# A graph attention and transformer kernel: masks moved to VectorE, the first product split in two parts, inputs in two buffers, edges written out in the loop's order

## The chip, the cores and the metric

The kernel runs on one core of a Trainium2 chip. TensorE (PE in the rows, PEld for its weight loads), VectorE (DVE), ScalarE (ACT), GpSimd (POOL) and SyncE (SP) each run their own stream of instructions in order and meet at semaphores. The metric is the device time of one execution, in microseconds (us); lower is better.

## What is computed

The input is a batch of 128 graphs of 128 nodes with 256 features. The first block is a graph attention with a top-16 filter, the second is three layers of graph attention with a feed-forward part of 1024 hidden units:

```python
h = jnp.maximum(_layernorm(x, axis=-1), 0.0)
x = x + _L0_gnn_ref(h, adj, W, a)
h = jnp.maximum(_layernorm(x, axis=-1), 0.0)
x = x + _L1_gnn_ref(h, adj, ...)

# _L0_gnn_ref
Wh = h @ W
e = leaky_relu((Wh @ a1)[:, :, None] + (Wh @ a2)[:, None, :], 0.2)
attention = softmax(where(adj > 0, e, -9e15))
attention = where(attention < 16th largest of its row, 0, attention)
return elu(attention @ Wh)

# _L1_gnn_ref, mask = adj + eye > 0, for each of three layers
scores = leaky_relu(si[:, :, None] + sj[:, None, :] + attn_b, 0.2)
attn = softmax(where(mask, scores, -inf))
h = layernorm(x + attn @ x) * g1 + beta1
x = layernorm(h + gelu(h @ W1 + b1) @ W2 + b2) * g2 + beta2
```

## The kernel before

**Tiling.** Four graphs make one group `k` (NG = 32 groups). A tile of scores is 128 x 512: the 128 nodes of four graphs side by side. For each group there is a first block (functions with `z_`, `e0`, `elu`) and three layers `l` of the second block. A pair (k, l) is a unit, and `seq(k, l)` is its number in the order of work: layer 1 of a group is worked one group behind layer 0, and layer 2 one more behind.

**Products in parts.** `mm1` (h @ W1, eight chunks `m` of 128 hidden units) and `mm2` (times W2) take float32r operands: each is split into a high part, rounded to float32r, and the low remainder, and three products are added: high by high, high by low, low by high. ScalarE makes the high part (`a_high`, `ht_high`), and the remainder comes from GpSimd for six of the eight chunks of `a_lo` and from VectorE for two (`LOW_ON_VECTOR = [3, 7]`) and for `ht_lo`. The product with W0 (`z_agg`) takes plain float32 operands, from `mixed`, which ScalarE copies out of PSUM in `mix_copy`. The aggregations (`agg`, `z_mix`) are plain float32 too.

**Masks.** `masks(k)` on VectorE makes two bf16 tiles with 0 or -2^100. One stays in SBUF for the first block; the other is parked in HBM by `park_mask` and loaded once for each layer by `load_mask`. The masks are added to the scores in PSUM, with a product by an identity at the end of `turn_sj` and `turn_e0`:

```python
pe.matmul(ps_s[:], ident_bf[:], mask_in[:, l].rearrange("p g m -> p (g m)"), start=False, stop=True, ...)
```

Then ScalarE forms a rectified copy (`leaky`), VectorE combines it with PSUM and takes the maximum (`scores_max`, `z_max`), ScalarE takes exponentials (`exps`), TensorE turns the result (`turn_p`, `turn_z`), and so on. `z_topk` finds the 16th largest value on VectorE before `turn_z`.

**Order.** Each engine has a function `iteration(i)`, an order written out by hand that works on pieces of groups i-3 to i+5. `schedule` calls it for i = -5 to 3 unrolled (the opening), for i = 4 to 25 in a loop on the chip whose body holds two iterations (11 turns), and for i = 26 to 34 unrolled (the closing). In the unrolled parts, pieces of groups that don't exist are left out. On TensorE one iteration holds 24 chunks of `mm1` and 24 of `mm2`, with the small products between them; `mm1` of a unit needs both halves of `ht_lo`, and `mm2` of chunk m needs that chunk's `a_lo`.

**Inputs.** `xr` is one buffer: `load_x(k)` waits until `elu_plus(k-1)` has read it. `zo` shares its memory with `hn0`, so `x0_norm(k)` waits for the first block's end for k-1. `elu_plus`, `elu_exp` and `elu_minus` work on all four graphs at once.

Of the kernel before, what the change touches and what calls it, by code (L numbers as in the profile page):

```python
# [12 lines left out]
P = 128  # L13
D = 256
# [12 lines left out]
FIRST, LAST = -5, NG + 3  # L27
# [55 lines left out]
def before_last(k, l):  # L83


    if isinstance(k, At):
        return seq(k, l) - 1
    at = L * k + (L + 1) * l - 1
    return sum(L * kk + (L + 1) * ll < at for kk in range(NG) for ll in range(L))
# [8 lines left out]
def chunks_before(k, l, m):  # L98


    c = seq(k, l) * MC + m
    if isinstance(k, At):
        return c - 2
    same = [seq(kk, ll) * MC + mm for kk in range(NG) for ll in range(L) for mm in range(MC) if (ll * MC + mm) % 3 == (l * MC + m) % 3]
    return max([n + 1 for n in same if n < c], default=0)
# [14 lines left out]
def build_program(nc, x, adj, W0, a0, attn_w, attn_b, W1, b1, W2, b2, g1, be1, g2, be2, out):  # L120
    ctx = ExitStack()
    with ctx:
# [8 lines left out]

        w1_hi = sb("w1_hi", [L, DC, HID], F32R)
# [3 lines left out]
        w0 = sb("w0", [DC, D])  # L136
# [12 lines left out]
        ident_bf = sb("ident_bf", [P], BF16)  # L149
# [14 lines left out]
        xr = sb("xr", [G, D])  # L164
# [23 lines left out]
        top = sb("top", [TOPK_ROUNDS, G, 8])  # L188
        w1_stage = X[:, 1:3].rearrange("p l g d -> p (l g d)").rearrange("p (c n) -> p c n", c=DC)
# [36 lines left out]
        CONSTS = 10  # L226
# [6 lines left out]
        def flat(ap):  # L233
            return ap.rearrange("p a n -> p (a n)")

        def schedule(iteration, eng):

            for i in range(FIRST, FIRST_STEADY):
                iteration(i)
# [3 lines left out]
            for i in range(LAST_STEADY + 1, LAST):  # L243
                iteration(i)
# [5 lines left out]
        def _(sp):  # L250
# [10 lines left out]
            sp.dma_start(xr[:], x_g[0]).then_inc(s["x_in"], 16)  # L261
            sp.dma_start(a0_row, row(a0.rearrange("n o -> (n o)"), 2 * D).rearrange("p (j d) -> p j d", j=2)).then_inc(s["a0_in"], 16)
# [1080 lines left out]
```

## Time and profile before

| | |
|---|---|
| median of 3 runs | 2915.42 us (2913.39 to 2915.62) |
| the profiled execution: its time, its span | 2913.98 us, 2912.3 us |
| mean granted TensorE clock | 0.986 of 2.4 GHz |
| busy: TensorE, its weight loads | 2752.7 us (95%), 2474.2 us (85%) |
| busy: VectorE, ScalarE, GpSimd | 2026.0 us (70%), 2350.6 us (81%), 2313.8 us (79%) |
| mean HBM traffic | 29 GB/s |

The span runs from the first to the last instruction; the time is 1.7 us longer. Busy shares are averages over the opening, the loop and the closing, which have different limits. Matmuls are pipelined: the duration of one in the rows holds its way through the array, and what it costs is the distance from its start to the next start. One float32 product of two operands appears as two MATMUL records, a float32r or bf16 product or a transpose as one.

### The profile page before, as it was taken

Reading aid. Unit: us, or ns where it says so; the run is one execution under the profiler, and the core shown is the slowest. Engines: PE = TensorE matmul, PEld = TensorE weight load, DVE = VectorE, ACT = ScalarE, POOL = GpSimd, SP = SyncE. Lnnn points to the kernel's source line nnn. Section 1 sums busy time; section 2 is a strip of 40 time slices with the busy share of each in tenths; the row PEclk is TensorE's granted clock in tenths of the full one; section 3 lists DMA queues with packets and bytes.
Section 4 is the critical chain, followed back from the end, with each engine's and each line's share of the span. In section 5 each row is a group of like instructions: output and inputs, shape, how many; then the busy total and the mean of one; then the engine's idle time right before and its main releaser. Section 6 shows DMA issues by size and latency. Waiting matters only on the chain.

```text
span 2912.3 us, 58716 instructions
## 1 busy us (share of the span) xinstructions
PE 2752.7 (95%) x17636; PEld 2474.2 (85%) x17636; DVE 2026.0 (70%) x7283; ACT 2350.6 (81%) x4767; POOL 2313.8 (79%) x2410
## 2 busy tenths in 40 slices
PE   4689999999999999999999999999999999999995
PEld 3578998888888898988889898888888999999874
DVE  4767777767777777777777777776777777676542
ACT  3577888888898888888888888888888888887663
POOL 0466888888888888888888888888888888888874
PEclk9899999999999999999999999999999999999997
DMA  4100011101101101101110110111110111010001
GB/s 150 46 28 26 25 34 25 34 20 34 33 27 25 35 20 34 34 26 34 25 35 20 34 32 28 25 34 20 34 35 25 34 25 34 20 30 19 10 10 15
DMA packets 96432, 89.72 MB, mean 31 GB/s; under 512 B 9120, under 2 KB 94368, under 8 KB 96032
## 3 DMA queue, kind: packets, MB, share of 16 engines
q1 hardware_dynamic: 79136, 68.32, 7.6%
q0 software_dynamic: 16896, 16.78, 4.4%
q8 instruction: 163, 2.67, 0.4%
q14 instruction: 237, 1.94, 0.2%
HBM read 47.34 MB, written 37.75 MB: 29 GB/s over the span
## 4 chain that ended last, share of the span: by engine, by line
PE 79%; DVE 12%; issue 4%; ACT 3%; POOL 1%; SPq 0%; DMA 0%; DVEq 0%; POOLq 0%; ACTq 0%
PE ps_ff L1120 11%; PE ps_ff L1122 10%; PE ps_ff L1121 10%; PE ps_mm L1101 10%; PE ps_mm L1099 10%; PE ps_mm L1100 10%; PE ps_ag L1157 5%; PE ps L1233 4%; PE ps_ht L1171 3%; PE ps L1223 2%; DVE U L893 1%; PE ps_s L1145 1%; DVE H L1005 1%; DVE st_y_six L789 1%; PE ps_s L1134 1%
## 5 line engine op out<-in xcount | busy, mean ns | idle before, releaser
L418 POOL TENSOR_TENSOR a_lo<-A,a_hi 128x512 fp32r<-128x512 f32 x576 | 776.1, 1350 | 347.3 <-ACT a_hi L541 334.9
L1120 PE MATMUL ps_ff<-w_hi,a_hi 128*128 128x256 f32 x3072 | 900.6, 293 | 26.3 <-DVE a_lo L995 14.6
L1121 PE MATMUL ps_ff<-w_lo,a_hi 128*128 128x256 f32 x3072 | 853.5, 278 | 0.0
L1122 PE MATMUL ps_ff<-w_hi,a_lo 128*128 128x256 f32 x3072 | 852.8, 278 | 0.0
L533 ACT ACTIVATE A<-ps_mm,b_col 128x512 f32<-128x512 f32 x768 | 521.7, 683 | 319.9 <-PE ps_mm L1101 191.9
L1099 PE MATMUL ps_mm<-ht_hi,w_hi 128*128 128x512 f32 x1536 | 630.8, 411 | 4.8 <-ACT A L533 3.4
L1120 PEld LDWEIGHTS ps_ff<-w_hi,a_hi 128*128 128x128 f32 x3072 | 577.4, 188 | 54.8 <-DVE a_lo L995 17.3
L1101 PE MATMUL ps_mm<-ht_lo,w_hi 128*128 128x512 f32 x1536 | 607.0, 395 | 0.0
L1100 PE MATMUL ps_mm<-ht_hi,w_lo 128*128 128x512 f32 x1536 | 604.2, 393 | 0.0
L1121 PEld LDWEIGHTS ps_ff<-w_lo,a_hi 128*128 128x128 f32 x3072 | 578.5, 188 | 18.4
L1122 PEld LDWEIGHTS ps_ff<-w_hi,a_lo 128*128 128x128 f32 x3072 | 578.1, 188 | 0.0
L541 ACT ACTIVATE a_hi<-A 128x512 fp32r<-128x512 f32 x768 | 478.2, 631 | 14.4
L935 DVE CUSTOM_DVE_ANT_0 junk<-X,wij_row 128x256 bf16<-128x256 f32 x768 | 342.5, 509 | 11.8 <-POOL X L442 6.7
L1101 PEld LDWEIGHTS ps_mm<-ht_lo,w_hi 128*128 128x128 f32 x1536 | 289.7, 189 | 62.4
L1099 PEld LDWEIGHTS ps_mm<-ht_hi,w_hi 128*128 128x128 f32 x1536 | 290.0, 189 | 54.6 <-ACT A L533 5.2
L1100 PEld LDWEIGHTS ps_mm<-ht_hi,w_lo 128*128 128x128 f32 x1536 | 290.7, 189 | 44.7
L986 DVE TENSOR_TENSOR ht_lo<-ps_ht,ht_hi 128x512 fp32r<-128x512 f32 x192 | 130.6, 680 | 259.9 <-ACT ht_hi L614 259.7
L425 POOL TENSOR_TENSOR H<-H,g_row 128x512 f32<-128x512 f32 x192 | 267.8, 1402 | 12.7 <-ACT H L547 12.3
L397 POOL TENSOR_TENSOR H<-X,g_row 128x512 f32<-128x512 f32 x192 | 261.8, 1377 | 17.9 <-DMA out<-H 9.8
L408 POOL TENSOR_TENSOR H<-H,bb_row 128x512 f32<-128x512 f32 x192 | 275.0, 1432 | 0.0
L1005 DVE TENSOR_TENSOR H<-ps_ff,H 128x512 f32<-128x512 f32 x192 | 123.0, 682 | 178.7 <-PE ps_ff L1122 176.9
L970 DVE SCALAR_TENSOR_TENSOR X<-ps_ag,a_rden,X 128x256 f32<-128x256 f32 x384 | 167.1, 476 | 105.7 <-PE ps_ag L1157 104.7
(113 smaller groups left out, 5129.8 us busy)
## 6 DMA issues: line engine op xcount, KB each, us to landing
xr<-in_x SPq DMA_DIRECT2D x32, 512.0 KB, 3.9
out<-x SPq DMA_DIRECT2D x32, 512.0 KB, 2.9
out<-H POOLq DMA_DIRECT2D x32, 512.0 KB, 6.1
mask_in<-mask_park SPq DMA_DIRECT2D x96, 128.0 KB, 2.4
adj_sb<-in_adj SPq DMA_DIRECT2D x32, 256.0 KB, 2.9
mask_park<-mask_out SPq DMA_DIRECT2D x32, 128.0 KB, 1.7
X<-in_L_gnn_W SPq DMA_DIRECT2D x3, 1024.0 KB, 5.7
H<-in_L_gnn_W SPq DMA_DIRECT2D x3, 1024.0 KB, 6.7
```

What stands on the lines that cost most here:

```text
L408: pool.tensor_tensor(H[:, l, two], H[:, l, two], bb_row[:, l:l + 1, :].to_broadcast([P, 2, D]), ALU.add).then_inc(s["h_res"], 1)
L418: pool.tensor_tensor(a_lo[:, at], A[:, at], a_hi[:, at].bitcast(F32), ALU.subtract).then_inc(s["a_lo_gpsimd"], 1)
L425: pool.tensor_tensor(H[:, l, two], H[:, l, two], g2_row[:, l:l + 1, :].to_broadcast([P, 2, D]), ALU.mult).then_inc(s["y_scaled"], 1)
L533: act.activation(A[:, (l * MC + m) % 3], ps_mm[m % 2][:], ACT.Gelu, bias=b1_col[:, l, m:m + 1]).then_inc(s["gelu_made"], 1)
L541: act.activation(a_hi[:, at], A[:, at], ACT.Copy).then_inc(s["a_hi_made"], 1)
L935: last = dve.tensor_tensor_reduce(out=junk[:, 2 * g + j], in0=X[:, l, g], in1=wij_row[:, l, j], scale=1.0, scalar=0.0, op0=ALU.mult, op1=A ...
L1099: pe.matmul(ps_mm[m % 2][:], w1_hi[:, l, d, cols], ht_hi[:, k % 2, d], start=(d == 0), stop=False)
L1100: pe.matmul(ps_mm[m % 2][:], w1_lo[:, l, d, cols], ht_hi[:, k % 2, d], start=False, stop=False)
L1101: last = pe.matmul(ps_mm[m % 2][:], w1_hi[:, l, d, cols], ht_lo[:, k % 2, d], start=False, stop=(d == DC - 1))
L1120: pe.matmul(out_g, a_hi[:, at, cols], w2_hi[:, l, m], start=first, stop=False, skip_group_check=True)
L1121: pe.matmul(out_g, a_hi[:, at, cols], w2_lo[:, l, m], start=False, stop=False, skip_group_check=True)
L1122: last = pe.matmul(out_g, a_lo[:, at, cols], w2_hi[:, l, m], start=False, stop=final, skip_group_check=True)
```

## The change

1. **Masks.** The mask products leave `turn_sj` and `turn_e0`, with `ident_bf`. Two new functions on VectorE, `scores_mask(k, l)` and `z_mask(k)`, add the mask in SBUF to the rectified copy, before `scores_max` and `z_max`.
2. **W0.** W0 is split once into `w0_hi` and `w0_lo`. `mix_copy` becomes `mix_high` (the same copy, into float32r), a new `mix_low` on VectorE makes the remainder from PSUM, and `z_agg` adds three float32r products.
3. **Inputs and aliases.** `xr` has two buffers; `load_x` runs one group further ahead. `z_out` writes into `x1`, so `x0_norm` no longer waits for the ELU. The ELU works in halves (`elu_exp(k, half)`, `elu(k, half)`). `kept` is also `pt0`, and serves as scratch with `U0`. Several global semaphores become one for each layer, and `moments` waits for the old coefficients before its first instruction and not before its second group.
4. **Buffers of units.** `ht_hi`, `ht_lo` and the ring of three `A`, `a_hi`, `a_lo` are now picked by the unit's number in the order of work. In the loop that gives the same choice.
5. **Order.** All engines have a new order in the loop, and the opening and the closing are written out (functions `opening` and `closing`) in nearly that order. The low parts stay split two to six. SP loads W0, a0, W2 and W1 of layer 0 ahead of x(0), and adj(0) comes after all constants and x(1); constants have three semaphores in place of one.

```diff
-                pe.matmul(ps_s[:], ident_bf[:], mask_in[:, l].rearrange("p g m -> p (g m)"), start=False, stop=True,
-                          skip_group_check=True).then_inc(s["sj_turned"], 1)
...
+            def scores_mask(k, l):
+                if not here(k):
+                    return
+                n = seq(k, l)
+                dve.wait_ge(s["scores_leaky"], value(n + 1))
+                dve.wait_ge(s_mask[l], value(k * 16 + 16))
+                tt(flat(U[:]), flat(U[:]), flat(mask_in[:, l]), ALU.add).then_inc(s["masked"], 1)
...
+            def z_mask(k):
+                if not here(k):
+                    return
+                dve.wait_ge(s["z_leaky"], value(k + 1))
+                dve.wait_ge(s["mask_made"], value(k * 2 + 1))
+                tt(flat(U0[:]), flat(U0[:]), flat(mask0[:]), ALU.add).then_inc(s["z_masked"], 1)
...
+            def mix_low(k, half):
+                if not here(k):
+                    return
+                dve.wait_ge(s["mix_hi_made"], value(k * 2 + half + 1))
+                tt(flat(mix_lo[:]), ps_0[:], flat(mix_hi[:]).bitcast(F32), ALU.subtract).then_inc(s["mix_split"], 1)
...
-                pe.wait_ge(s["mix_copied"], value(k * 2 + half + 1))
+                pe.wait_ge(s["mix_split"], value(k * 2 + half + 1))
                 for g in range(2):
...
-                        last = pe.matmul(ps_0[:, g * D:(g + 1) * D], mixed[:, c, g * P:(g + 1) * P], w0[:, c],
-                                         start=(g == 0 and c == 0), stop=(g == 1 and c == DC - 1), skip_group_check=True)
+                        pe.matmul(out_g, mix_hi[:, c, rows], w0_hi[:, c], start=(g == 0 and c == 0), stop=False, skip_group_check=True)
+                        pe.matmul(out_g, mix_hi[:, c, rows], w0_lo[:, c], start=False, stop=False, skip_group_check=True)
+                        last = pe.matmul(out_g, mix_lo[:, c, rows], w0_hi[:, c], start=False, stop=(g == 1 and c == DC - 1),
+                                         skip_group_check=True)
```

The order in the loop, where the prediction speaks of it (k = i+2 has its first block in this iteration):

```diff
 TensorE, from the end of layer 1's mm2 to turn_z and z_agg:
                 mm2(i - 1, 1, 7)
-                mm1(i - 2, 2, 1)
                 mm1(i - 2, 2, 2)
                 mm1(i - 2, 2, 3)
+                turn_sj(i, 1)
                 mm2(i - 2, 2, 0)
                 mm1(i - 2, 2, 4)
+                mm1(i - 2, 2, 5)
                 mm2(i - 2, 2, 1)
                 turn_z(i + 2)
-                mm1(i - 2, 2, 5)
+                turn_h(i + 1, 0, 0)
+                mm2(i - 2, 2, 2)
                 z_mix(i + 2, 0)
-                turn_h(i + 1, 0, 0)
                 mm1(i - 2, 2, 6)
                 z_agg(i + 2, 0)
 VectorE, the same stretch:
                 y_sum(i - 1, 1)
                 y_moments(i - 1, 1)
-                z_recip(i + 2)
                 z_topk(i + 2)
+                z_recip(i + 2)
+                a_low(i - 2, 2, 3)
+                scores_mask(i, 1)
+                ht_low(i + 1, 0, 0)
                 scores_max(i, 1)
-                a_low(i - 2, 2, 3)
-                ht_low(i + 1, 0, 0)
+                mix_low(i + 2, 0)
+                recip(i, 1)
                 z_out(i + 2, 0)
 VectorE, the end of an iteration and (after the bar) the start of the next:
-                ht_low(i, 1, 0), y1_sum(i - 1, 2, 0), ht_low(i, 1, 1) | scores_max(i + 2, 0), y1_sum(i - 1, 2, 1)
+                ht_low(i, 1, 0) | y1_sum(i - 1, 2, 0), scores_mask(i + 2, 0), scores_max(i + 2, 0), ht_low(i, 1, 1)
 TensorE, the same place:
-                mm2(i + 1, 0, 7), mm1(i, 1, 2), mm1(i, 1, 3) | mm2(i, 1, 0)
+                turn_h(i, 1, 1), agg(i - 1, 2, 1), mm2(i + 1, 0, 5) | mm1(i, 1, 0), mm1(i, 1, 1)
```

## Rows read from the trace of the kernel before

**Rows 1.** The page: busy time (share) xinstructions, and the chain that ended last.
```profile
PE 2752.7 (95%) x17636; PEld 2474.2 (85%) x17636; DVE 2026.0 (70%) x7283; ACT 2350.6 (81%) x4767; POOL 2313.8 (79%) x2410
...
PE 79%; DVE 12%; issue 4%; ACT 3%; POOL 1%; SPq 0%; DMA 0%; DVEq 0%; POOLq 0%; ACTq 0%
```

**Rows 2.** Windows: length; busy (x) of PE, PEld, DVE, ACT, POOL; PEclk, DMA share, GB/s.
```profile
0.00:103.00 103.00, 49.63 (x205) 41.48 (x206) 55.50 (x188) 36.99 (x74) 14.67 (x29) 0.95 0.40 123
103.00:300.00 197.00, 169.75 (x1021) 147.85 (x1020) 139.70 (x535) 142.19 (x304) 122.43 (x138) 0.92 0.09 28
...
616.00:2250.00 1634.00, 1602.85 (x10422) 1448.29 (x10420) 1195.91 (x4316) 1395.26 (x2834) 1383.34 (x1425) 1.00 0.12 29
2250.00:2586.00 336.00, 335.38 (x2186) 303.81 (x2184) 245.28 (x906) 292.16 (x595) 287.61 (x301) 1.00 0.12 29
2586.00:2912.30 326.30, 283.36 (x1784) 251.14 (x1782) 157.40 (x511) 210.10 (x409) 240.56 (x242) 0.93 0.09 14
```

**Rows 3.** Timeline of PE in a loop group: `turn_z`, `z_agg`, `mm2`. Start, length (us).
```profile
1501.04 0.66 PE L1210 MATMUL ps<-ident,U 128*128 128x128 f32 x4 [0.72 <-DVE U L893]
1501.45 0.48 PE L1099 MATMUL ps_mm<-ht_hi,w_hi 128*128 128x512 f32 x1
...
1505.65 1.89 PE L1233 MATMUL ps<-w,mixed 128*128 128x256 f32 x8
...
1507.49 0.28 PE L1121 MATMUL ps_ff<-w_lo,a_hi 128*128 128x256 f32 x1
...
1510.00 0.28 PE L1122 MATMUL ps_ff<-w_hi,a_lo 128*128 128x256 f32 x1
```

**Rows 4.** Timeline of PE in another loop group: a mask product.
```profile
1561.09 0.38 PE L1202 MATMUL ps<-mask,ident_bf 128*128 128x512 bf16 x1
...
1561.43 0.28 PE L1121 MATMUL ps_ff<-w_lo,a_hi 128*128 128x256 f32 x1
```

**Rows 5.** Waits in the loop (616 to 2250): us in total, times, longest.
```profile
PEld ps L1210 <- DVE U L893: 16.0, 19, 1.0
...
PE ps_ff L1120 <- DVE a_lo L995: 12.2, 9, 1.5
...
PE ps_ff L1120 <- issue: 6.4, 9, 1.0
```

**Rows 6.** Groups of DVE in the loop: busy us, mean ns.
```profile
L970 DVE SCALAR_TENSOR_TENSOR X<-ps_ag,a_rden,X 128x256 f32<-128x256 f32 x230 | 100.0, 475 | 57.8 <-PE ps_ag L1157 57.8
L995 DVE TENSOR_TENSOR a_lo<-A,a_hi 128x512 fp32r<-128x512 f32 x115 | 91.1, 792 | 33.9 <-ACT a_hi L541 33.4 <-PE ps_ff L1122 0.5
...
L986 DVE TENSOR_TENSOR ht_lo<-ps_ht,ht_hi 128x512 fp32r<-128x512 f32 x114 | 77.4, 679 | 134.4 <-ACT ht_hi L614 134.4
```

**Rows 7.** Three lines by source: duration ns min/median/max.
```profile
L995 DVE TENSOR_TENSOR a_lo<-A,a_hi x192: 656/692/1857, 117.0 to 2889.4; 128x512 fp32r<-128x512 f32 x192
...
L986 DVE TENSOR_TENSOR ht_lo<-ps_ht,ht_hi x192: 655/682/693, 97.0 to 2866.1; 128x512 fp32r<-128x512 f32 x192
...
L418 POOL TENSOR_TENSOR a_lo<-A,a_hi x576: 1256/1300/1829, 108.6 to 2889.0; 128x512 fp32r<-128x512 f32 x192
```

**Rows 8.** Timeline of DVE: the chain to `turn_z`, and the loop's branch.
```profile
1114.24 0.29 DVE L949 CUSTOM_DVE_ANT_0 U<-ps_s,U 128x128 f32<-128x128 f32 x1 [2.46 <-issue]
...
1492.08 1.29 DVE L1005 TENSOR_TENSOR H<-ps_ff,H 128x512 f32<-128x512 f32 x2 [3.45 <-PE ps_ff L1122]
...
1498.82 2.16 DVE L893 SCALAR_TENSOR_TENSOR U<-U,top 128x128 f32<-128x128 f32 x4
```

**Rows 9.** Chain that ended last, in the opening: the first weights.
```profile
16.05 7.07 DMA X<-in_L_gnn_W
23.17 7.00 PE ps_ht L1180 x32
```

**Rows 10.** Timeline of ACT in the opening.
```profile
42.63 1.91 ACT L521 ACTIVATE w_hi<-H 128x2048 fp32r<-128x2048 f32 x1 [1.86 <-DMA H<-in_L_gnn_W]
44.45 0.58 ACT L656 ACTIVATE pt<-ps 128x512 f32<-128x512 f32 x1
```

More of the change, by code:

```diff
@@ L65, in here @@
     return isinstance(k, At) or 0 <= k < NG
+UNITS = sorted(((k, l) for k in range(NG) for l in range(L)), key=lambda u: L * u[0] + (L + 1) * u[1])
 def seq(k, l):
@@ L72, in seq @@
         return k * L + ((L + 1) * l - L)
-    at = L * k + (L + 1) * l
-    return sum(L * kk + (L + 1) * ll < at for kk in range(NG) for ll in range(L))
+    return UNITS.index((k, l))
 def earlier(k, l):
@@ L83, in before_last, with ht_at, a_at @@
 def before_last(k, l):
[L86 to L89, printed above, removed]
+    return seq(k, l) - 1 if isinstance(k, At) else max(seq(k, l) - 1, 0)
+def ht_at(k, l):
+    return k % 2 if isinstance(k, At) else (seq(k, l) + 1) % 2
+def a_at(k, l, m):
+    return ((L + 1) * l * MC + m) % 3 if isinstance(k, At) else (seq(k, l) * MC + m) % 3
 def ready(k, l):
@@ L101, in chunks_before @@
     c = seq(k, l) * MC + m
[L102 to L105, printed above, removed]
+    return c - 2 if isinstance(k, At) else max(c - 2, 0)
 def some(n):
@@ L219, in build_program @@
         s_w2 = [sem(f"w2_in{l}") for l in range(L)]
+        s_xin = [sem(f"x_in{p}") for p in range(2)]
         s_mask = [sem(f"mask_in{l}") for l in range(L)]
@@ L231, in row, with schedule @@
             return ap.rearrange("(o n) -> o n", o=1).to_broadcast([P, n])
[L233 to L239, printed above, removed]
+        def schedule(opening, iteration, closing, eng):
+            opening()
             with eng.Fori(0, (LAST_STEADY + 1 - FIRST_STEADY) // 2) as j:
@@ L242, in schedule @@
                 iteration(At(j, 2, FIRST_STEADY + 1))
-            for i in range(LAST_STEADY + 1, LAST):
-                iteration(i)
+            closing()
         block = ctx.enter_context(nc.Block())
@@ L338, in _ @@
+            schedule(opening, iteration, closing, sp)
             sp.wait_ge(s["out_added"], 16 * NG)
@@ L509, in _ @@
+            schedule(opening, iteration, closing, pool)
         @block.scalar
@@ L714, in iteration @@
                 a_high(i - 1, 1, 1)
+                p_copy(i + 1, 0)
                 h_norm(i - 2, 2)
@@ L762, in _ @@
+            schedule(opening, iteration, closing, act)
         @block.vector
@@ L902, in z_out @@
                 dve.wait_ge(s["z_agg"], value(n + 1))
-                for g in range(2):
-                    j = 2 * half + g
-                    last = ts(zo[:, j], ps_0[:, g * D:(g + 1) * D], zrden[:, j:j + 1], None, ALU.mult)
-                last.then_inc(s["z_out_made"], 1)
-            def elu_plus(k):
-                if not here(k):
-                    return
-                dve.wait_ge(s["z_out_made"], value(k * 2 + 2))
                 if some(k):
@@ L1083, in _ @@
+            schedule(opening, iteration, closing, dve)
         @block.tensor
         def _(pe):
-            pe.wait_ge(s["const_made"], 5)
+            pe.wait_ge(s["const_made"], 4)
             def mm1(k, l, m):
@@ L1323 @@
+            schedule(opening, iteration, closing, pe)
 _INS = ["x", "adj", "L0_gnn_W", "L0_gnn_a", "L1_gnn_attn_w", "L1_gnn_attn_b", "L1_gnn_W1", "L1_gnn_b1",
```

3148 lines of the change are left out of this document (2885 added, 263 removed).

## The prediction

> **What bounds the kernel now.** I read the page first: TensorE is busy 95% of the span and makes 79% of the chain that ended last; VectorE, ScalarE and GpSimd are at 70, 81 and 79% [rows 1]. An average hides the stages, so next the windows, cut at starts of `turn_e0` [rows 2]. The loop from 616 to 2250 us holds 19 groups, 86.0 us each, and PE is idle in 31 us of 1634. The four unrolled groups after it take 84.0 us each with 0.6 us idle. The first 300 us leave PE idle for 53 + 27 us and the last 326 us for 43. So in the loop the time is TensorE's own work, and what TensorE loses is lost at the edges. ScalarE and GpSimd are 85% busy in the loop (1395 and 1383 of 1634), VectorE 73%: 63 us a group.
>
> The third view is PE's timeline, because a matmul's duration is not its cost. `mm2` products start 0.114 us apart (22 steps from 1507.49 to 1510.00) [rows 3]. A mask product with one `mm2` product behind it takes from 1561.09 to 1561.43, 0.34 us, so it costs 0.226 us [rows 4]. One half of `z_agg`, eight float32 records, with one `mm2` product behind it takes from 1505.65 to 1507.49, 1.84 us, so it costs 1.73 [rows 3].
>
> The fourth is the list of waits in the loop [rows 5]. PE's queue waits for VectorE before `turn_z` in every one of the 19 groups, 16.0 us in all (0.84 each), and at nine loop turns for an `a_lo` of VectorE (12.2 us) and for its own branch ("issue", 6.4 us).
>
> **What the change takes from TensorE.** (a) Four mask products a group, three layers and the first block, 128 in all: 128 x 0.226 = 28.9 us. (b) `z_agg`: eight float32 records become twelve float32r products of the shape that `mm2` has, 12 x 0.114 = 1.37 us in place of 1.73. 64 halves x 0.36 = 23.0 us. Together 51.9 us, 1.6 us a group. TensorE is the bound in 27 groups, and at the edges these pieces stand in the chain as well, so I count all of it. From below it could be worth 27/32 of that, 44 us.
>
> **What it puts on VectorE.** Four mask adds a group, 128x512 with both inputs in SBUF. The nearest row is the `a_lo` remainder, also from SBUF: mean 0.79 us, from 0.66 to 1.86 [rows 6, 7]. I take 0.8, bounds 0.66 and 1.86. Two `mix_low` a group, one input in PSUM, as `ht_lo`: 0.68, never over 0.69 [rows 6, 7]. Sum 4 x 0.8 + 2 x 0.68 = 4.6 us a group; the ELU in halves adds a few tenths. VectorE goes from 63 to 68 us in a period of about 84, 80%. Hidden behind TensorE as long as no step that TensorE waits for comes later than its place in the order.
>
> The spread of that `a_lo` row needs a reason: the same subtraction with one input in PSUM keeps to 0.655 to 0.693, with both in SBUF it reaches 1.857, and GpSimd's own `a_lo` reaches 1.829 over a median of 1.300 [rows 7]. So the mask adds will sometimes wait for GpSimd, and GpSimd for them. The Trainium skill (SBUF — State Buffer, "SBUF: two separate sides") says that VectorE with two SBUF inputs and GpSimd share a port pair as an exclusive lock, the loser blocked for the whole instruction. The trace agrees with a blocking of about one such operation at most. By that rule an add behind a whole `a_lo` of GpSimd (1.30) would take 1.96, and four of them a group 7.8 us in place of my 3.2; that is taken up in the second rival.
>
> **What moves in the loop.** (c) `turn_z`. From the start of `y_sum` at 1492.08 to the end of `z_topk` at 1500.98, VectorE runs without a gap to speak of, 8.9 us, and PE waits for its end [rows 3, 8]. The y_sum itself starts when `mm2(i-1,1,7)` ends. Between that and `turn_z` the new order has the same six units of `mm1` and `mm2` and now also the four transposes of `turn_sj` (0.41 us, the distance from 1501.04 to 1501.45 [rows 3]), and `z_recip` (0.14) comes after `z_topk`. So the wait of 0.84 falls to about 0.3: 0.5 x 31 groups = 16 us off. Bounds 0 and 0.84. (d) `z_agg(0)` now waits for two steps, `mix_high` and then `mix_low`, and one `mm1` chunk (about 1.4 us) stands between. From `z_mix`'s last start: 0.3 through the array (the rest of its duration), 0.58 on ScalarE as `z_copy` [rows 10], 0.68 on VectorE, small hops, about 1.7; PE covers 1.4. A wait of 0.3 x 31 = 9 us on, bounds 0 and 1 each if `scores_max`, which stands ahead of `mix_low`, is late. The second half has 5 us of cover. (e) The loop's turn. VectorE stands idle 2.46 us at its branch [rows 8]. Before, that fell after both `ht_lo` of the unit; now it falls between them, with `y1_sum` (2 x 0.475 less overlap, 0.87 [rows 6]), a mask add (0.8) and `scores_max` (about 1) ahead of the second. From the first `ht_lo`'s start: 0.7 + 2.5 + 0.9 + 0.8 + 1 + 0.7 = 6.6 us, PE's cover (two `mm2` chunks, transposes, `agg`, one `mm2` chunk, less ScalarE's lead) some 5. A wait of 1.6 at each of 11 turns, where before 12.2 + 6.4 over 9 turns gave 2.1 [rows 5]. PE's own branch has shorter work queued ahead, which can eat the difference. I take 0, bounds -10 and +20 us.
>
> SP: `load_adj(i+3)` now stands behind `load_x(i+4)`, which waits for the ELU late in iteration i. `masks` follows in the next iteration after more than ten operations, so the adjacency has time to land. `store_x1` and the mask loads stand behind waits that were met an iteration earlier. I cost them at nothing; if the cover went, `masks` and behind it VectorE's whole order would be late by a transfer, 3 to 5 us a group.
>
> **The edges.** Before, the first weights are issued at 16.05, land at 23.1, and their 32 bias products hold PE to 30.2, ahead of the first `turn_e0` [rows 9]; then `z_copy` stands behind `w2_high(1)`, which ends at 44.5, some 3 us after `turn_z` [rows 10]. Now W1 and W2 are issued ahead, but x(0) behind 2.5 MB and adj(0) behind some 6 MB. At the rate of the first weights and constants I put adj(0) near 23 us, so the first `turn_e0` comes about where it was, and only the 3 us of `w2_high(1)` are won: -3 us, bounds -12 and +8. In the dependent stretches of opening and closing, some eight turns of the score chain stand open to PE, and each is longer by a mask add less a mask product (0.6) or two `mix_low` less 0.7: +6 us, bounds 2 and 12.
>
> **The sum.** Span 2912.3 - 51.9 (a, b) - 16 (c) + 9 (d) + 0 (e) - 3 + 6 = 2856.4; with 1.7 around it 2858. The runs' median is 1.4 above the profiled execution's 2913.98. I add 2 us for small waits as VectorE fills up and say **2861 us**, 1.9% faster.
>
> **The rivals.**
> *The new order takes out more.* PE's idle time in the loop (31 us) mostly goes and the opening wins its 12 us: 2861 - 15 - 9 - 5 = 2832. For it: each wait in the list has a cause that an order can mend. Against it: the branches stay.
> *VectorE's new work shows.* The mask add sits in the chain `leaky`, add, `scores_max`, `exps`, `turn_p`, and PE takes `turn_p` at a fixed place. If the adds are blocked by GpSimd (1.86 each) and half of 4 x 1.86 + 2 x 0.68 = 8.8 us a group reaches PE in 27 groups, that is +119: 2980; a quarter gives 2921, slower than before. It decides at 57/27 = 2.1 us of new waits a group. Against it: no wait of PE for `exps` is among those of the loop, and VectorE has 23 us of slack a group.
> *Most is given back.* (d) costs 1 us a group (+22), the loop's turn +20, opening +8: about 2900.
> *No change.* The three products of `z_agg` don't start 0.114 apart and the mask products were free. Against it: [rows 3, 4] show both prices on PE's own clock of starts. 2912.
>
> **How the numbers follow.** Forecast 0.55, more taken out 0.18, given back 0.13, VectorE shows 0.11 (0.02 of it within 0.2%), no change 0.03. A measurement of this kernel tells some 0.2%, 6 us, from nothing. Faster 0.55 + 0.18 + 0.13 = 0.86, same 0.02 + 0.03 = 0.05, slower 0.09. The range leaves out a little at each end: from the low case less 4, 2828, to the given-back case, 2900. The likeliest case alone is 2842 to 2880.
>
> **What would show it.** In the trace after: no bf16 matmuls; `z_agg` at 0.114 a product; windows of the loop near 84.3 us a group, PE busy still over 97%; VectorE near 80%; `turn_z` waiting 0.3 us or less for VectorE, a new wait of 0.2 to 0.4 at `z_agg`; mask adds of 0.7 to 0.9 mean with a tail to 1.9. Wrong if PE waits for `exps` or `ht_lo` in each group, or if the first `mm1`, at 103 us before, starts after 110.

## The result, and the profile after

The changed kernel took 3005.6 us (median, 3003.5 to 3007.1) beside 2914.4 us for the kernel before: a ratio of 1.0314, 95% interval 1.0301 to 1.0327, so 3.1% slower. The prediction was 2861 us, faster, with a range of 2828 to 2900. The profiled execution took 3003.48 us with a span of 3001.7.

The page of the kernel after, the lines that answer [rows 1]: busy time and the chain.

```profile
PE 2760.5 (92%) x17764; PEld 2459.4 (82%) x17764; DVE 2231.2 (74%) x7574; ACT 2366.1 (79%) x4800; POOL 2295.3 (76%) x2409
...
PE 41%; DVE 21%; issue 14%; POOL 10%; ACT 10%; DMA 0%; DVEq 0%; POOLq 0%; ACTq 0%
```

TensorE was 79% of the chain and is 41%. The time is no longer TensorE's own work. That its busy time has not fallen by the 52 us says little, because behind a wait a matmul's record is longer: 0.49 us for the `mm1` product that ends a wait at 1693.00, 0.40 for its like at 1693.80. Where the waits are gone, the busy time does fall with the work moved: 2763.4 us in z4, 2722.4 in z2 (two runs below that differ by that work alone).

Windows of the kernel after. The last three are cut at the same starts of `turn_e0` as in [rows 2]; the first two end at the first `mm1` (106, before 103) and at the fifth `turn_e0` (290, before 274), so the second has no partner in [rows 2] (length; busy of PE, PEld, DVE, ACT, POOL; clock; DMA; GB/s).

```profile
0.00:106.00 106.00, 49.90 (x219) 44.65 (x220) 57.60 (x199) 37.76 (x77) 10.84 (x28) 0.98 0.40 121
106.00:290.00 184.00, 145.94 (x856) 126.79 (x856) 131.21 (x477) 120.90 (x262) 103.03 (x116) 0.88 0.10 30
...
638.00:2324.00 1686.00, 1607.96 (x10490) 1434.10 (x10489) 1319.91 (x4484) 1402.91 (x2850) 1370.68 (x1426) 0.99 0.12 28
2324.00:2667.00 343.00, 334.80 (x2207) 300.50 (x2207) 279.38 (x944) 295.09 (x601) 285.47 (x301) 1.00 0.12 27
2667.00:3001.70 334.70, 286.00 (x1790) 252.75 (x1788) 168.56 (x526) 214.67 (x414) 241.23 (x244) 0.93 0.09 14
```

The 19 groups of the loop take 1686 us against 1634 (88.7 each against 86.0), the four behind it 343 against 336, the closing 8 us more, and the loop's window begins 22 us later. VectorE is busy 69.5 us a group in the loop (1319.9 / 19), about the 68 forecast.

TensorE's waits in the loop, 638 to 2324 us (us in total, times, longest), to be read against [rows 5], and VectorE's wait before `recip`. [rows 5] has the wait of `turn_z` on the weight loads' row (PEld), 16.0 us; on the row of the products (PE), as here, the kernel before had 12.2 us in the same 19 groups.

```profile
PE ps_mm L3043 <- issue: 22.8, 14, 2.9
PE ps_ff L3066 <- DVE a_lo L2403: 16.3, 13, 1.3
PE ps_ag L3101 <- DVE X L2378: 14.0, 25, 1.2
PE ps_ff L3066 <- POOL a_lo L507: 6.8, 12, 0.7
PE ps L3152 <- DVE U L2289: 5.4, 9, 1.2
...
PE ps L3178 <- DVE mix_lo L2297: 3.3, 5, 0.7
```

```profile
DVE a_rden L2368 <- ACT U L1198: 58.9, 29, 2.8
```

The wait of `turn_z` (L3152) fell as forecast. Three others came: for TensorE's own branch, for `a_lo`, and at `agg` for `y1_sum` (L2378). And VectorE, the engine that got more to do, stands idle 58.9 us before `recip` in the loop, where the kernel before lost 2.8 us in the whole run.

How a branch reaches TensorE: VectorE, then TensorE, at one turn of the loop (start, length, idle before).

```profile
1685.04 0.69 DVE L2394 TENSOR_TENSOR ht_lo<-ps_ht,ht_hi 128x512 fp32r<-128x512 f32 x1 [1.79 <-ACT ht_hi L1216]
1688.14 0.88 DVE L2378 SCALAR_TENSOR_TENSOR X<-ps_ag,a_rden,X 128x256 f32<-128x256 f32 x2 [2.41 <-issue]
```

```profile
1689.07 1.13 PE L3101 MATMUL ps_ag<-X,pt 128*128 128x256 f32 x4 [1.11 <-DVE X L2378]
...
1693.00 0.49 PE L3043 MATMUL ps_mm<-ht_hi,w_hi 128*128 128x512 f32 x1 [1.42 <-issue]
...
1695.79 0.50 PE L3043 MATMUL ps_mm<-ht_hi,w_hi 128*128 128x512 f32 x1 [1.13 <-issue]
```

VectorE is idle 2.41 us at its branch, as it was before (2.46) [rows 8]. Behind it stands a `y1_sum` that `agg` waits for, so the loss reaches TensorE at once. Then TensorE stands idle twice more, 1.42 and 1.13 us before `mm1`, and waits for nothing that the profile shows. I read both as its own branch: with the loop written out (y5 below) this row is gone.

### The profile page after: what moved, and what is told of

It is laid out like the page before. It is cut to its first block, busy times and chain, and to the rows that moved or that the text cites. A ratio compares the mean times of both kernels' runs of the same rounds, so it can differ in the third digit from the quotient of the medians.

```text
span 3001.7 us, 59533 instructions
## 1 busy us (share of the span) xinstructions
PE 2760.5 (92%) x17764; PEld 2459.4 (82%) x17764; DVE 2231.2 (74%) x7574; ACT 2366.1 (79%) x4800; POOL 2295.3 (76%) x2409
## 4 chain that ended last, share of the span: by engine, by line
PE 41%; DVE 21%; issue 14%; POOL 10%; ACT 10%; DMA 0%; DVEq 0%; POOLq 0%; ACTq 0%
PE ps_ff L3066 6%; PE ps_ff L3067 6%; PE ps_ff L3068 6%; PE ps_mm L3043 5%; DVE junk L2335 5%; PE ps_mm L3045 5%; PE ps_mm L3044 5%; PE ps_ag L3101 3%; POOL a_lo L507 3%; ACT H L1150 2%; ACT a_hi L1144 2%; DVE X L2378 2%; DVE st_h_six L2178 2%; ACT A L1136 2%; POOL H L497 1%
## 5 line engine op out<-in xcount | busy, mean ns | idle before, releaser
L3066 PE MATMUL ps_ff<-w_hi,a_hi 128*128 128x256 f32 x3072 | 887.0, 289 | 44.4 <-DVE a_lo L2403 26.1
L3043 PE MATMUL ps_mm<-ht_hi,w_hi 128*128 128x512 f32 x1536 | 630.1, 410 | 41.0 <-issue 24.6
L2335 DVE CUSTOM_DVE_ANT_0 junk<-X,wij_row 128x256 bf16<-128x256 f32 x768 | 342.2, 508 | 17.3 <-POOL X L531 12.2
L2403 DVE TENSOR_TENSOR a_lo<-A,a_hi 128x512 fp32r<-128x512 f32 x192 | 196.3, 1022 | 156.5 <-ACT a_hi L1144 146.6
L497 POOL TENSOR_TENSOR H<-H,bb_row 128x512 f32<-128x512 f32 x192 | 253.3, 1325 | 10.0 <-DVE bb_row L2166 9.9
L1150 ACT ACTIVATE H<-H,st_y_nmr,st_y_rstd 128x256 f32<-128x256 f32 x384 | 198.7, 590 | 56.9 <-POOL st_y_nmr L450 56.9
L3101 PE MATMUL ps_ag<-X,pt 128*128 128x256 f32 x768 | 209.8, 396 | 28.0 <-DVE X L2378 23.0
```

Source lines behind the costliest of these rows:

```text
L497: pool.tensor_tensor(H[:, l, two], H[:, l, two], bb_row[:, l:l + 1, :].to_broadcast([P, 2, D]), ALU.add).then_inc(s_res[l], 1)
L2335: last = dve.tensor_tensor_reduce(out=junk[:, 2 * g + j], in0=X[:, l, g], in1=wij_row[:, l, j], scale=1.0, scalar=0.0, op0=ALU.mult, op1=A ...
L3043: pe.matmul(ps_mm[m % 2][:], w1_hi[:, l, d, cols], ht_hi[:, ht_at(k, l), d], start=(d == 0), stop=False)
L3066: pe.matmul(out_g, a_hi[:, at, cols], w2_hi[:, l, m], start=first, stop=False, skip_group_check=True)
L3101: last = pe.matmul(ps_ag[:, g * D:(g + 1) * D], pt[:, j * P:(j + 1) * P], X[:, l, j], start=(g == 0), stop=(g == 1), skip_group_check=True)
```

## The experiments

Medians in us, ratio to runs of the kernel before on the same chip with its 95% interval. "Old" is the kernel before, "new" the kernel after, with the edit named.

| run | edit | time | ratio |
|---|---|---|---|
| x1 | old + masks and W0 as after | 3031.2 | 1.0399 (1.0382 to 1.0417) |
| x2 | new, masks and W0 as before | 3004.5 | 1.0309 (1.0292 to 1.0326) |
| x3 | old + masks alone | 3050.5 | 1.0472 (1.0454 to 1.0489) |
| x4 | old + W0 alone | 2948.3 | 1.0123 (1.0106 to 1.0140) |
| y5 | new, loop written out | 2931.6 | 1.0062 (1.0046 to 1.0079) |
| y6 | old, loop written out | 2875.4 | 0.9872 (0.9856 to 0.9888) |
| y7 | new, branch moved | 2981.0 | 1.0231 (1.0214 to 1.0248) |
| y8 | new, `recip` late | 2985.1 | 1.0242 (1.0225 to 1.0259) |
| z1 | new, branch moved, `recip` late | 2942.9 | 1.0097 (1.0081 to 1.0114) |
| z2 | new, written out, `recip` late | 2879.1 | 0.9878 (0.9862 to 0.9894) |
| z3 | old + masks, written out | 2924.4 | 1.0026 (1.0008 to 1.0044) |
| z4 | z2, masks and W0 as before | 2903.7 | 0.9964 (0.9954 to 0.9975) |
| w1 | new, masks added in PSUM | 2991.6 | 1.0267 (1.0242 to 1.0292) |
| w2 | x3, masks added in PSUM | 2953.5 | 1.0137 (1.0119 to 1.0154) |
| w3 | z2, masks in PSUM, one step of the opening | 2866.8 | 0.9843 (0.9827 to 0.9860) |
| w4 | z1, masks in PSUM | 2946.5 | 1.0122 (1.0105 to 1.0139) |
| v1 | old, masks in PSUM, W0, written out | 2911.3 | 1.0002 (0.9993 to 1.0011) |
| v2 | v1 with the loop | 2952.4 | 1.0135 (1.0114 to 1.0156) |

### Work or order: x1 to x4

x1 puts the added work into the old order (here the masks; `mix_low` and the split of W0 likewise), x2 takes it out of the new one.

```diff
 x1, VectorE
+                scores_mask(i + 1, 0)
                 scores_max(i + 1, 0)
...
+                mix_low(i + 2, 0)
                 ht_low(i + 1, 0, 0)
...
                 ht_low(i + 1, 0, 1)
+                mix_low(i + 2, 1)
```

> The kernel before, its order unchanged, with the masks added on VectorE (each add directly ahead of its maximum) and W0 in high and low parts (the low part of the first half ahead of ht_low(i+1,0,0), the second behind ht_low(i+1,0,1)). Theory Work (VectorE's new instructions are what TensorE waits for): the 52 us taken from TensorE come back as waits of the size seen after the change, about 4 us a group, so 2914 - 52 + 27 x 4.4 = 2980, at least 2940. Theory Order (the new order of the steps makes the waits): the work is nearly hidden as forecast, 2914 - 52 + 20 for waits of the score chain and of z_agg = 2882, at most 2900.

> The kernel after, with its order, buffers and edges, but the masks added by products on TensorE again and W0 in plain float32 (no scores_mask, z_mask, mix_low). Theory Work: without the new instructions on VectorE the waits go, and the time is that of the kernel before or a little less, 2895 to 2920. Theory Order: TensorE has 52 us more to do and waits as it did after the change, so 3005 + 52 less what the longer TensorE work covers (about half): 3030, at least 2990.

> The kernel before with the masks alone on VectorE; W0 stays float32. Theory Work, if the mask adds carry it (they lie in the score chain and are blocked by GpSimd's port): 2914 - 29 + 27 x 3 = 2966, above 2930. Theory Order: 2914 - 29 + some 10 = 2895.

> The kernel before with W0 in two parts alone; masks stay products on TensorE. Forecast of term (b) and (d): 2914 - 23 + 9 = 2900 by both theories; under 2895 if the wait of z_agg is covered in the old order, over 2915 if ht_low behind mix_low is late for mm1.

Neither theory stands alone. In the old order the work costs 117 us, above what theory Work said; and the new order costs 90 us with the old work. Together they cost 91, not 207: in the new order the new work is free of cost (3004.5 against 3005.6), but free of gain too. In x2 VectorE stands idle 89 us before `recip` in the 19 groups of the loop, so that wait comes with the order and not with the work. x3 came out on theory Work's side, but 84 us above its number: the masks alone cost 137 us. W0 alone costs 34 where 14 were to be won; the time is in the range that x4 gave to a late `ht_low`, but TensorE waits for `mix_low` there, as shown below.

TensorE's waits of x3 between 616 and 2290 us show where (the rows of [rows 5] for this kernel).

```profile
PE ps_ff L1137 <- DVE a_lo L1008: 34.9, 28, 2.8
PE ps L1223 <- DVE U L898: 30.3, 9, 3.7
PE ps_ff L1137 <- issue: 18.5, 10, 2.1
```

The count 9 is that of the loop's turns in this window: `turn_z` waits up to 3.7 us for VectorE once a turn and not in the groups between. From one `turn_e0` to the next, x3 takes 98 us in a group with a turn, 85 in one without and 85 to 86 behind the loop.

### The loop's branch: y5, y6, y7, z3

```diff
 y5, y6, z3: schedule
-            with eng.Fori(0, (LAST_STEADY + 1 - FIRST_STEADY) // 2) as j:
-                iteration(At(j, 2, FIRST_STEADY))
-                iteration(At(j, 2, FIRST_STEADY + 1))
+            for i in range(FIRST_STEADY, LAST_STEADY + 1):
+                iteration(i)
 y7: VectorE, first calls of the body moved to its end (TensorE: seven calls, up to mm1(i - 1, 1, 3))
-                y1_sum(i - 2, 2, 0)
-                scores_mask(i + 1, 0)
-                scores_max(i + 1, 0)
-                ht_low(i - 1, 1, 1)
                 y1_sum(i - 2, 2, 1)
...
                 ht_low(i, 1, 0)
+                y1_sum(i - 1, 2, 0)
+                scores_mask(i + 2, 0)
+                scores_max(i + 2, 0)
+                ht_low(i, 1, 1)
```

> The kernel after with its loop on the chip written out: the same calls in the same order for i = 4 to 25, no branch. In the trace after, the groups with a loop turn take about 92.6 us from turn_e0 to turn_e0 and the four behind the loop 85.3. Theory Turn (an overfull VectorE can't make good what it loses at its branch): the turn's excess of 7.3 us goes 11 times, 3005 - 80 = 2925, at most 2945. Theory Spread (the waits are those of every group, the turn only moves them): at least 2980.

> The kernel before with its loop written out. Its groups with a turn take 87.1 us, the others 84.9 in the loop and 84.1 behind it, so 11 x 3.0 + 11 x 0.8 = 42 off by the four groups behind the loop: 2872; at least 11 x 2.2 = 24 off: 2890. Theory Turn expects the gap of the two written-out kernels to be 2925 - 2872 = 53 us or less, against 91 with the loops; theory Spread the same 91.

> The kernel after with the loop's branch at the place in the order where it was before: on VectorE behind ht_low(i,1,1), on TensorE behind mm1(i,1,3). The order of the instructions is unchanged. If the new place of the branch makes the turn dear (term (e), put at 0 with an upper bound of 20): some 5 of the 7.3 us a turn come back, 3005 - 55 = 2950. If the turn is dear wherever it stands, since VectorE has no slack behind it to catch up: 2990 to 3010; the masks alone in the old order, with the branch at its old place, speak for that.

> The old order with the masks on VectorE (3050 with the loop), the loop written out. Its groups with a turn took 98 us, the four behind the loop 84.9 to 86. Theory Turn: 3050 - 11 x 13 = 2907, which is 2875 and some 30. Theory Spread (blocked adds cost in every group): at least 2950.

Eleven turns of the loop cost 74 us after (3005.6 - 2931.6) and 39 before (2914.4 - 2875.4). The gap of the two kernels falls from 91 to 56. From one `turn_e0` to the next, the kernel after takes 92.5 us in a group with a turn and 85.3 in one without, and y5 takes 85.3 in all, so the price is paid where the branch is. The kernel before has 87.2 and 84.9, y6 has 84.2. Written out, a kernel also loses the loop's counter and address instructions (y5 has 55,386 instructions, the kernel after 59,533), and no run separates these from the branch. "Branch" stands for both below.

With the branch at its old place 25 us come back (y7), half of what was expected, so the place is a part of it. With the masks in the old order the turns cost 126 us (3050.5 - 2924.4), 87 more than without; theory Turn put z3 17 us too low, and 49 us over y6 remain without a branch. The eight executions of z3 spread over 27 us (2908.8 to 2936.1), so these numbers are good to some 10 us.

Windows from the fifth `turn_e0` to the last (27 groups), and behind it: y5, then y6.

```profile
288.50:2590.80 2302.30, 2259.13 (x14906) 2028.18 (x14905) 1886.24 (x6372) 1992.12 (x4050) 1924.18 (x2023) 1.00 0.12 29
2590.80:2923.50 332.70, 283.24 (x1787) 250.46 (x1785) 167.09 (x526) 214.15 (x413) 241.31 (x244) 0.94 0.09 14
```

```profile
273.20:2545.40 2272.20, 2271.65 (x14799) 2058.18 (x14798) 1658.74 (x6130) 1974.89 (x4024) 1945.25 (x2025) 1.00 0.12 29
2545.40:2868.70 323.30, 280.13 (x1785) 248.64 (x1783) 156.97 (x511) 210.23 (x409) 240.25 (x242) 0.95 0.09 14
```

Without branches the old kernel is TensorE alone, 84.2 us a group with 0.5 us idle in 27 groups. The new one has less to do there and takes 85.3, with 43 us idle. The edges are 15.3 + 9.4 us longer.

### The wait for the exponentials: y8, z1, z2, z4

```diff
 y8, z1, z2, z4: VectorE, in the opening, the loop and the closing
-                recip(i + 1, 0)
                 masks(i + 2)
                 y_sum(i, 0)
...
+                recip(i + 1, 0)
                 y1_sum(i + 1, 0, 0)
```

> The kernel after with each recip(k, l) directly ahead of y1_sum(k, l, 0) and not ahead of z_out, masks and y_sum, in the opening, the loop and the closing. VectorE waits 58 us for exps there in the loop. If these waits (the order) reach TensorE, half of them come back, 3005 - 40 = 2965. If the added work carries it, VectorE only waits elsewhere: 2995 to 3010.

> The kernel after with both single edits: the branch at its old place on VectorE and TensorE (alone 25 us off) and recip directly ahead of y1_sum (alone 20 us off). If the two are different causes they add: 3005 - 25 - 20 = 2960. If both only give VectorE back the same slack: no better than 2975. If a VectorE with no idle time for exps recovers from its branch as fast as before (3 us a turn): 2940.

> The kernel after with the loop written out (alone 2931) and recip directly ahead of y1_sum. In the run with recip late the groups behind the loop take 83.8 us against 85.3: 2931 - 27 x 1.4 = 2893. If the wait for exps is covered where no branch is: 2925.

> The new order with the old work (mask products on TensorE, W0 in float32), written out and with recip late: it differs from the kernel after with the same two edits by the moved work alone. If terms (a) and (b) hold where no branch and no early recip stand in the way: that kernel's time + 52 - 10 = about 2935. If VectorE's new work gives it all back even here: the same time, 2893.

What it takes away, in VectorE's timeline of the kernel after, behind the loop:

```profile
2531.64 0.18 DVE L2368 RECIPROCAL a_rden<-a_den 128x4 f32<-128x4 f32 x1 [2.79 <-ACT U L1198]
2531.82 0.88 DVE L2310 TENSOR_SCALAR x<-ps,z_rden 128x256 f32<-128x256 f32 x2
```

`recip` needs the exponentials (L1198) and only `y1_sum`, some operations on, needs `recip`; `z_out`, `node_scores` and `ht_low` stand behind it meanwhile. How it reaches TensorE: the wait for `a_lo` in 19 groups without a branch, y5 (638 to 2240 us), then z2 (616 to 2290).

```profile
PE ps_ff L3065 <- DVE a_lo L2402: 18.3, 19, 1.1
```

```profile
PE ps_ff L3065 <- DVE a_lo L2402: 0.6, 1, 0.6
```

Moved, `recip` is worth 20 us with the loop (y8), 38 with the branch moved too (y7 to z1), and 52.5 written out (y5 to z2). So the branch hides a part of the gain. A turn does not become cheaper by it: the eleven cost 106 us with `recip` late (y8 against z2) and 74 without, and at the old place 64 (z1 against z2) and 49 (y7 against y5). One cause can be read in y8: the moved `recip` is now the first call of the body, behind the branch, `y1_sum` waits for it there, and `agg` waits 22.6 us in the loop in place of 14.0. In z1 both stand ahead of the branch, and the two edits together give 63 us, more than 20 + 25.

y8 missed its 40 us by half. z1 fell on the number of its third expectation (2940), but that one wanted turns of 3 us and they cost 5.8, so the number was met by luck. z2 beat its own by 14 us, and z4 lies between its two.

z4 and z2 differ by the moved work alone. Windows of the 27 groups: z4, then z2, then w3 of the next part.

```profile
284.40:2565.70 2281.30, 2280.19 (x14797) 2060.48 (x14796) 1612.10 (x6210) 1992.58 (x4051) 1892.15 (x2023) 1.00 0.12 29
```

```profile
288.50:2544.10 2255.60, 2242.33 (x14905) 2025.13 (x14904) 1807.42 (x6372) 1987.52 (x4051) 1926.36 (x2023) 1.00 0.12 29
```

```profile
287.00:2531.20 2244.20, 2238.64 (x14906) 2025.89 (x14905) 1728.88 (x6372) 1989.50 (x4051) 1899.39 (x2024) 1.00 0.12 29
```

The moved work is worth 24.6 us (2903.7 - 2879.1), and 0.95 us a group (84.5 to 83.5), of the 1.6 that terms (a) and (b) take from TensorE. With unblocked adds (w3) it is 1.4.

z4 against y6 shows the rest of the change, since both do the old work without a branch and without an early `recip`: 2903.7 against 2875.4, 28 us more. By the profiled spans 9 us of it lie in the 27 groups (2281.3 against 2272.2) and 22 in the edges. So no run shows the new order ahead of the old one at the same work.

### The port: w1 to w4

```diff
-                tt(flat(U[:]), flat(U[:]), flat(mask_in[:, l]), ALU.add).then_inc(s["masked"], 1)
+                tt(ps_s[:], ps_s[:], flat(mask_in[:, l]), ALU.add).then_inc(s["masked"], 1)
...
-                tt(flat(U0[:]), flat(U0[:]), flat(mask0[:]), ALU.add).then_inc(s["z_masked"], 1)
+                tt(ps_0[:], ps_0[:], flat(mask0[:]), ALU.add).then_inc(s["z_masked"], 1)
 w3, the opening
-                w2_low(2)
                 mix_low(1, 1)
+                w2_low(2)
```

> The kernel after, but scores_mask and z_mask add the mask to the scores in PSUM (in place, behind the rectified copy) and not to the copy in SBUF; scores_max adds the two as before, so the sum is the same. The adds then have one SBUF input. After the change they took 0.91 (96) and 1.49 us (32), with a minimum of 0.67. Theory Port (they are blocked while GpSimd works, and block it): each takes 0.67 to 0.70 with no tail, VectorE gets back 96 x 0.22 + 32 x 0.8 = 47 us, and 3005 falls to 2960 to 2975. Theory Count (it is the number of instructions and their places, not the blocking): 2995 to 3010.

> The old order with the masks alone on VectorE (3050), the adds done in PSUM. There the score adds took 1.34 us each in the run with both edits. Theory Port: VectorE gets back about 96 x 0.65 + 32 x 0.4 = 75 us, most of it within 30 us behind the branch, so the 13 us that a turn costs fall to 6: 3050 - 80 = 2970 or less. Theory Count: 3030 to 3050.

> The kernel after, written out, recip late (2879), with the adds in PSUM, and in the opening mix_low(1,1) ahead of w2_low(2), for which z_agg waited 2.4 us there. Theory Port: the groups fall from 83.5 us to TensorE's 82.9, 27 x 0.6 = 16 off, the opening 3 to 5 off: 2860. Theory Count: 2875.

> The kernel after with its loop, the branch at its old place and recip late (2943), the adds in PSUM. Theory Port: the turn's 4 us fall to 2 and the groups by 0.6: 2943 - 22 - 16 = 2905. Theory Count: 2935 to 2943.

By source, min/median/max in ns. The kernel after: `z_mask`, `scores_mask`, `mix_low`, `a_low` on VectorE.

```profile
L2249 DVE TENSOR_TENSOR U<-U,mask x32: 673/1624/1659, 33.0 to 2671.2; 128x512 f32<-128x512 f32 x32
...
L2348 DVE TENSOR_TENSOR U<-U,mask_in x96: 662/691/1793, 73.8 to 2932.9; 128x512 f32<-128x512 f32 x96
...
L2297 DVE TENSOR_TENSOR mix_lo<-ps,mix_hi x64: 675/684/693, 45.7 to 2708.9; 128x512 fp32r<-128x512 f32 x64
...
L2403 DVE TENSOR_TENSOR a_lo<-A,a_hi x192: 654/693/1823, 124.0 to 2979.6; 128x512 fp32r<-128x512 f32 x192
```

`scores_mask` in the old order, in SBUF (x3) and in PSUM (w2):

```profile
L953 DVE TENSOR_TENSOR U<-U,mask_in x96: 684/1548/1877, 74.9 to 2980.2; 128x512 f32<-128x512 f32 x96
```

```profile
L953 DVE TENSOR_TENSOR ps_s<-ps_s,mask_in x96: 673/700/700, 74.7 to 2896.5; 128x512 f32<-128x512 f32 x96
```

With one input in PSUM the tail is gone. In the old order that alone takes 97 us off (w2), so most of what the masks cost there was GpSimd's blocking. In the new order the score adds were mostly unblocked already (median 691), and it is worth 14 us in w1, whose four executions spread over 21, 12 with a step of the opening (w3), and nothing measurable in w4. So the port explains x3, and only a small part of the kernel after. `z_mask` was blocked nearly always, here by a bias operation of GpSimd, which is then late itself: VectorE, then GpSimd, of the kernel after.

```profile
2586.19 1.53 DVE L2249 TENSOR_TENSOR U<-U,mask 128x512 f32<-128x512 f32 x1
```

```profile
2585.88 1.29 POOL L524 TENSOR_TENSOR H<-H,be_row 128x512 f32<-128x512 f32 x1
2587.13 1.73 POOL L531 TENSOR_TENSOR X<-H,be_row 128x512 f32<-128x512 f32 x1
```

The add ends 0.55 us after the GpSimd operation that had begun before it, and the next one of GpSimd takes 1.73 us where its median is 1.29. The Trainium skill (SBUF — State Buffer, "SBUF: two separate sides") has this rule, a lock on the pair of ports held for a whole instruction, between a GpSimd operation that reads SBUF and a VectorE operation with two SBUF inputs; w2 agrees, with 700 ns at most for an add that has one.

### The old order once more: v1, v2

```diff
 v1, v2: the kernel before with W0 and the masks in PSUM; v1 written out. TensorE:
+                mm2(i - 2, 2, 2)
                 z_agg(i + 2, 0)
-                mm2(i - 2, 2, 2)
```

> The old order, buffers and edges, written out, with the masks added by VectorE in PSUM, W0 in two parts, and z_agg(i+2,0) one chunk of mm2 later, so that its wait of 2 us for mix_low is covered. Written out, the old kernel took 2875 with TensorE at 84.1 us a group. If TensorE keeps what is taken from it (1.6 us a group) where the adds are not blocked, no branch stands in the way and the edges are the old ones: 2875 - 27 x 1.4 = 2837; if, as in the new order, half is given back: 2855. Not better than 2867 (the best of the new order) if the new order is what makes the moved work fit.

> The same kernel with the loop. The masks in PSUM alone took 2953, of which some 11 x 6 for the turns beyond those of before. The turn should stay dear, at about 9 us against 2.3 to 3 before, even with unblocked adds: v1 + 80 = 2920 to 2940. If the turn becomes as cheap as before: v1 + 38 = 2875 to 2890.

Both missed. TensorE's waits of v1 between 616 and 2290 us have one row, and VectorE's timeline in one group says why:

```profile
PE ps L1265 <- DVE mix_lo L913: 35.9, 20, 1.8
```

```profile
1002.73 0.47 DVE L996 SCALAR_TENSOR_TENSOR X<-ps_ag,a_rden,X 128x256 f32<-128x256 f32 x1
1003.12 0.68 DVE L1012 TENSOR_TENSOR ht_lo<-ps_ht,ht_hi 128x512 fp32r<-128x512 f32 x1
1003.71 0.68 DVE L913 TENSOR_TENSOR mix_lo<-ps,mix_hi 128x512 fp32r<-128x512 f32 x1
```

The cover was put before the wrong half. It is the second `z_agg` that waits, 1.8 us in each of 20 groups, for a `mix_low` that stands behind `ht_low` and `y1_sum`. The same wait is in x4 (28.7 us in 19 groups), where it carries most of what W0 alone lost. So v1 doesn't show what the old order could do with that wait mended, and whether it would beat w3 is open. The 41 us between v1 and v2 are again the branch: 3.7 us a turn, near the 3.5 of the kernel before and far from the 11.5 with blocked adds, as the second expectation of v2 had it for the difference.

## Why the prediction was wrong, step by step

**The sum that the runs give.** 91.2 us = 35.0 (the branch: 74.0 against 39.0) + 52.5 (`recip` ahead of its need, y5 to z2) + 3.7 (all the rest, z2 against y6: by the windows 28 us of longer edges less 17 won in the groups, and the medians lie closer than these two profiled spans). The split depends on the order of removal, because a turn is dearer with `recip` late. The other way round, `recip` gives 20.5 (to y8) and the branch 67.0 (106.0 against 39.0), with the same 3.7 left. The sum of the two, 87.5, is measured either way; the share of each depends on the order.

Against the forecast of 2861 the miss is 145 us: the branch 35.0; `recip` 52.5; 27 of the 52 us of terms (a) and (b) that did not come (z4 to z2 gave 24.6); and about 30 for the order and the edges, which cost 28 (z4 against y6) where terms (c), (d), the edges and the 2 us for small waits came to -2.

**The step that failed** is the sentence that VectorE's load was "hidden behind TensorE as long as no step that TensorE waits for comes later than its place in the order", with its 23 us of slack a group. The load was right, 69.5 us a group. But slack was counted over a period and not at places. The diff had two things in plain sight that use it up: `recip(i, 1)` ahead of `z_out` and not behind it as before, which the prediction never priced (52.5 us between y5 and z2), and the branch, priced in (e).

**Term (e)**, the loop's turn, was 0 with bounds of -10 and +20; it is +35. Its working followed one chain, to the second `ht_low`. In the trace the turn is paid at `mm1` (22.8 us) and at `agg` (14.0 in the loop, 7.0 without a branch), and behind them for GpSimd's `a_lo` (6.8) and at `turn_z` (5.4), rows that y5 doesn't have. The wait for VectorE's `a_lo` (16.3) isn't the branch's: it is 18.3 us in y5 and goes with the early `recip`. The Trainium skill (Runtime: NRT & Kernel Launch, "Instruction fetch mechanics") warns that a taken branch stalls the fetch and that unrolling is preferred; y6 agrees, 39 us in 11 turns in an already tuned kernel.

**Terms (a) and (b)** had the right price. The twelve products of a `z_agg` half take 1.42 us from start to start, forecast 1.37 (PE, a group behind the loop):

```profile
2625.41 0.28 PE L3178 MATMUL ps<-w_hi,mix_hi 128*128 128x256 f32 x1
...
2626.83 0.40 PE L3043 MATMUL ps_mm<-ht_hi,w_hi 128*128 128x512 f32 x1
```

What failed was counting all of it: with branch and early `recip` removed, half was kept (z4 to z2, 24.6 of 52).

**VectorE's new instructions.** `mix_low` 0.68 us as forecast. The mask adds were put at 0.8 each; the four of a group took 0.91 three times and 1.49 once (87.2 / 96 and 47.6 / 32 us), 1.05 on average, within the bounds.

**Term (c)** was right in kind: `turn_z` waits 5.4 us in 9 groups in place of 12.2 in 19, or 7.1 in place of 16.0 on the weight loads' row that the prediction read. **Term (d)** too: `z_agg` waits 3.3 us in the loop on PE, 12.0 on the weight loads' row (19 times). The two about cancel, where -16 and +9 were put down. In the old order, with `mix_low` where x4 has it, it is 28.7; so the new order did this part well.

**The edges** were put at +3 and are about +25 (y5 against y6). One delay that the trace shows: in the opening, `w2_low(2)` stands ahead of `mix_low(1, 1)`.

```profile
103.69 0.58 PE L3178 MATMUL ps<-w_hi,mix_hi 128*128 128x256 f32 x1 [2.40 <-DVE mix_lo L2297]
104.07 0.41 PE L3179 MATMUL ps<-w_lo,mix_hi 128*128 128x256 f32 x1
104.29 0.41 PE L3180 MATMUL ps<-w_hi,mix_lo 128*128 128x256 f32 x1
```

```profile
103.60:109.00 5.40, 5.30 (x19) 4.73 (x20) 3.08 (x7) 0.00 (x0) 1.28 (x1) 0.50 0.01 3
```

TensorE had just stood idle for 2.40 us; from there its granted clock is 0.50 of 2.4 GHz for 5.4 us, the lower of its two levels, and products start 0.21 apart and not 0.11. The kernel before had 1.00 over the same stretch, but 0.74 from 95 to 100 us. The delay is worth little: w3, which has that step mended, reaches the fifth `turn_e0` at 287.0 us, z2 at 288.5, y6 at 273.2. Most of it is in the new order itself: x2, with the old work, already reaches the fifth `turn_e0` 11 us later than before. Which step of the opening and of the closing does it was not tried; it stays open.

**The rivals.** "VectorE's new work shows" had the right sign and, for the old order, the right mechanism (x3, w2). It was given 0.11 on the ground that no wait of TensorE for `exps` was among those of the loop, and on the 23 us of slack. The first spoke of TensorE's rows in the old order; in the new one it is VectorE that waits for `exps`, at `recip`. The time of 3005.6 lies above all four rivals, the dearest of which was 2980.

**Also open:** why the branch still costs 80 us in the new order with all three mends (w4 against w3, which differ in the opening's step and the branch alone), against 39 before and 41 in v2, which has the moved work in the old order. In w4 `turn_z` waits 22.6 us in 19 groups and `a_lo` 13.7, so VectorE is late for the rest of the body; what fills it there was not separated.

**A version that beats both** is w3 at 2866.8 us (0.9843), the changed kernel written out with `recip` late and masks added in PSUM. The kernel before merely written out has 2875.4 (0.9872); the intervals touch, and nearly all of the gain is the missing branch.

## What to carry to other kernels

Count an engine's slack at each place where another waits for it, never as busy share of a period; and in a new order look first for an instruction that waits for a third engine while its own result is needed later, since all that stands behind it pays. The same branch cost 3.5 to 11.5 us a turn here, by what stood behind it and how full VectorE was, so price it again for each change of load, and try a loop written out when its body is full. If VectorE has to take an addition beside a busy GpSimd, give it an operand in PSUM.

## What was not expected of the hardware

A branch of 2.4 us on VectorE cost the whole kernel 3.5 us a turn before, 6.7 after, 11.5 with blocked masks in the old order and 3.7 there with the masks in PSUM and W0 split. An add with both inputs in SBUF took up to 1.88 us beside GpSimd, and 0.70 at most with one in PSUM, worth 97 us in 3050.
